# Local attention in a transformer stack: dividing the probabilities ahead of their transposes, and weighing with the values stationary

## The chip, the cores and the metric

One core of a Trainium2 chip runs the whole program in one launch. The metric is the device time of one execution in microseconds (us); several executions give a median.

## The reference

The input x has 2048 tokens of 128 features in float32. The program computes x + 0.5 F(norm(x)), adds a linear-attention block of 16 heads with its own feed-forward part, and then adds 0.5 F again. F is a stack of 6 layers, run twice with the same weights, so there are 12 layer passes. What matters here is the attention of such a layer, with 16 heads of 64 dimensions and windows of 32 tokens, each of which looks at itself and at the window before:

```python
qkv = x @ Wqkv                      # x: tokens, its upper 64 features shifted by one token
q, k, v = sh(q), sh(k), sh(v)       # 16 heads of 64
q = l2norm(q) * qs; k = l2norm(k) * ksc
q, k = rotary(q), rotary(k)
sim = einsum('bhwie,bhwje->bhwij', bq, bk2) * 8.0   # 32 queries against 64 keys
attn = softmax(where(mask, -max, sim), -1)
out = einsum('bhwij,bhwje->bhwie', attn, bv2)
x = out.reshape(b, n, 1024) @ Wo + x
```

Behind it stand a layer norm, a gated feed-forward part of 341 hidden units, and a residual.

## The kernel before

Activations live in SBUF for the whole run with features on partitions (XA, XB: 128 x 2048). A layer's attention works through 16 chunks (CH) of 128 tokens. It is pipelined by hand over steps: in step i every engine's function `step(p, i, ...)` does part a for chunk i (projection), part b for chunk i-1 (rotation, scores), part cc for the chunk whose scores are now complete (softmax, transposes of the probabilities, first weighing) and part d for the chunk before (rest of weighing, output projection). Chunks 0 to 2 start the layer without all parts, and steps 16 to 18 (`within`, `norm_before`) end it with parts b, cc, d alone, beside the layer norm of the feed-forward part that follows. The order on each engine is written out in these functions, and engines meet at semaphores that count chunks: `wait_ge(name, c(k))`. `dve.drain()` makes VectorE wait for its own writes.

The parts that the change and the prediction speak of, by engine:

- TensorE (PE): `project` multiplies the chunk's tokens, split in a high and a low part (XH, XL), by the split weights, three passes for each half of q, k, v (L382 to L384). It needs XL (`xs_ready`). `turn` makes 128x128 transposes (L390): of V (the rotated q and k), of PR (the probabilities; lines 492 to 499, both in banks TQ and TK), and of ON (the divided result; line 458). `score` gives the logits of two heads of a pair (r = 0, 1), four windows each (L406). `weigh` multiplies the transposed probabilities PT by the values V2: the probabilities are loaded, the values stream, and the result has tokens on partitions, in bank OB for r = 0 and OB + 1 for r = 1 (L416). Its eight head pairs stand in four blocks of two: 0 to 3 in the step of the transposes around the last half of the value projection, 4 to 7 in the next step around the first projection. The output projection multiplies OT by WO (L466).
- ScalarE (ACT), in this order in a step: copy and square of q (L697, L699, RAWQK and SQ), the copy of the transposed result OT (L732), copy and square of k, the copies of the transposed q and k (QT L703, KT L706), the exponential (L743, PR from SM), the second copies, the halo of the keys, the copies of the transposed probabilities PT (L755, L756, wait for `pt_ready`), XH of the next chunk (`shift`, L692 and L693), the values VS (L710).
- VectorE (DVE), in this order: the division of the weighed result by the probabilities' sums (L968, ON), the second product of the rotation (`rotate(1)`, L934), the sum of squares of q (L950), the row maximum and its subtraction (MX L979, SM L981), the sum of squares of k, the residual (XB, L988), the inverse norms by a short iteration on 32 columns (L871 to L890), QN (L927, twice), XL of the next chunk (`rest`, L943 and L945, wait for XH), the sums of the probabilities (L998) and their reciprocals (L1002), the first product of the rotation (`rotate(0)`, L934).
- GpSimd (POOL): the other products of the rotation, four on QN (L1185), and two additions (L1191, L1193) that need DVE's `rotate(0)` and `rotate(1)`.
- SyncE (SP): weights, and the 16 copies of a chunk's values into V2, where each window has its own 64 keys.

## Time and profile before

| | |
|---|---|
| median of 2 runs | 4887.01 us (4881.81 and 4892.21) |
| span of the profiled execution, first to last instruction | 4869.5 us |
| TensorE matmul busy | 3785.1 us, 78% |
| VectorE busy | 3828.5 us, 79% |
| ScalarE busy | 2483.4 us, 51% |
| GpSimd busy | 2389.1 us, 49% |
| mean granted TensorE clock | 0.905 of 2.4 GHz |

All durations of the profile come from one profiled execution, whose time is known by its span alone; the median of the runs lies 17.5 us above that span. In rows, "x4" is the number of merged instructions, and brackets hold the idle time of the engine before the row with what ended it. Matmuls are pipelined, so rows of PE overlap.

### The profile page before, as it was taken

What the parts mean: (1) busy time and instruction counts of PE and PEld (TensorE: products, weight loads), DVE (VectorE), ACT (ScalarE), POOL (GpSimd) and SP (SyncE); (2) the same over time, 40 slices, a digit from 0 to 9 for tenths busy, and PEclk for the clock granted to TensorE, in tenths of its full rate; (3) what the DMA queues carried; (4) which work ended last, traced back from release to release, by engine and by line L of the source; (5) the groups of instructions that cost most, each with busy time, mean ns of one, the idle gap of its engine ahead of it and who ended that gap; (6) DMA issues with size and microseconds to landing.
All of it is one profiled execution on the core that took longest, in us unless ns stands there. A gap on an engine that the chain in (4) does not pass through costs nothing.

```text
span 4869.5 us, 152986 instructions
## 1 busy us (share of the span) xinstructions
PE 3785.1 (78%) x64080; PEld 2581.5 (53%) x64080; DVE 3828.5 (79%) x6082; ACT 2483.4 (51%) x3705; POOL 2389.1 (49%) x1426
## 2 busy tenths in 40 slices
PE   5887887787787787788777877877877887887887
PEld 3554554554555455456435645554554554554554
DVE  4886886896896897797448878877976886986896
ACT  3554554554554565455225545554554554553553
POOL 3663563563664564455006535544553653553552
PEclk9998899899899999888878989999988998998999
DMA  2221221221221222122002212221221221221221
GB/s 82 54 57 46 53 55 48 53 54 44 58 56 51 49 57 58 40 55 63 6 10 51 57 47 51 56 57 43 57 58 39 55 59 40 57 55 44 53 57 46
DMA packets 179337, 247.34 MB, mean 51 GB/s; under 512 B 52516, under 2 KB 75040, under 8 KB 177184
## 3 DMA queue, kind: packets, MB, share of 16 engines
q1 hardware_dynamic: 178976, 242.09, 19.6%
q8 instruction: 281, 4.60, 0.4%
q14 instruction: 80, 0.66, 0.0%
HBM read 39.51 MB, written 1.05 MB: 8 GB/s over the span
## 4 chain that ended last, share of the span: by engine, by line
PE 35%; POOL 18%; DVE 17%; ACT 10%; issue 8%; DVEq 7%; SPq 3%; DMA 1%; ACTq 0%; POOLq 0%
POOL V L1185 9%; PE PS L390 6%; PE PS L544 5%; POOL V L1191 5%; POOL V L1193 5%; PE PS L382 4%; PE PS L466 3%; PE PS L416 3%; DVEq L1000 3%; DVE QN L927 3%; PE PS L383 2%; PE PS L384 2%; DVEq L921 2%; PE PS L576 2%; ACT PR L743 2%
## 5 line engine op out<-in xcount | busy, mean ns | idle before, releaser
L1185 POOL TENSOR_TENSOR V<-QN,TAB 128x512 f32<-128x512 f32 x768 | 1116.7, 1485 | 1791.2 <-DVE QN L927 1791.2
L382 PE MATMUL PS<-WH,XH 128*128 128x512 f32 x1152 | 634.4, 551 | 427.8 <-DVE XL L945 338.8
L697 ACT ACTIVATE RAWQK<-PS 128x1024 f32<-128x1024 f32 x384 | 392.3, 1022 | 848.5 <-PE PS L384 808.1
L934 DVE TENSOR_TENSOR U<-QN,TAB 128x1024 f32<-128x1024 f32 x384 | 736.8, 1922 | 16.4 <-issue 15.3
L390 PE MATMUL PS<-EYE,V 128*128 128x128 f32 x3072 | 449.6, 285 | 188.0 <-POOL V L1193 107.8
L1191 POOL TENSOR_TENSOR V<-V,U 128x1024 f32<-128x1024 f32 x192 | 516.6, 2690 | 81.3 <-DVE U L934 60.8
L382 PEld LDWEIGHTS PS<-WH,XH 128*128 128x128 f32 x1152 | 241.5, 210 | 560.4 <-DVE XL L945 210.3
L1193 POOL TENSOR_TENSOR V<-V,U 128x1024 f32<-128x1024 f32 x192 | 453.6, 2362 | 140.4 <-DVE U L934 140.4
L390 PEld LDWEIGHTS PS<-EYE,V 128*128 128x128 f32 x3072 | 366.1, 147 | 276.6 <-POOL V L1193 139.8
L384 PE MATMUL PS<-WL,XH 128*128 128x512 f32 x1152 | 511.2, 444 | 0.0
L383 PE MATMUL PS<-WH,XL 128*128 128x512 f32 x1152 | 511.0, 444 | 0.0
L950 DVE TENSOR_REDUCE SS<-SQ 128x16 f32<-128x1024 f32 x384 | 463.9, 1209 | 23.6 <-ACT SQ L699 23.6
L927 DVE TENSOR_TENSOR QN<-RAWQK,RN 128x1024 f32<-128x1024 f32 x384 | 453.4, 1222 | 15.1 <-issue 0.4
L703 ACT ACTIVATE QT<-PS 128x512 f32<-128x512 f32 x384 | 229.4, 597 | 460.6 <-PE PS L390 460.6
L416 PEld LDWEIGHTS PS<-V,PT 64*32 64x32 f32 x24576 | 264.3, 118 | 372.8 <-issue 372.8
L416 PE MATMUL PS<-V,PT 64*32 64x64 f32 x24576 | 388.3, 244 | 85.1 <-issue 80.1
L466 PE MATMUL PS<-OT,WO 128*128 128x128 f32 x3072 | 417.3, 292 | 35.1 <-ACT OT L732 29.3
L466 PEld LDWEIGHTS PS<-OT,WO 128*128 128x128 f32 x3072 | 379.3, 201 | 67.6 <-ACT OT L732 67.5
L699 ACT ACTIVATE SQ<-RAWQK 128x1024 f32<-128x1024 f32 x384 | 406.9, 1060 | 12.2
L406 PE MATMUL PS<-KT,QT 64*32 64x64 f32 x24576 | 388.9, 233 | 2.6 <-issue 2.6
L968 DVE TENSOR_TENSOR ON<-PS,SUM 128x1024 f32<-128x1024 f32 x192 | 235.2, 1225 | 161.8 <-PE PS L416 153.5
L732 ACT ACTIVATE OT<-PS 128x1024 f32<-128x1024 f32 x192 | 197.0, 1026 | 309.5 <-PE PS L390 309.5
(150 smaller groups left out, 6509.1 us busy)
## 6 DMA issues: line engine op xcount, KB each, us to landing
V<-VS SPq DMA_DIRECT2D x3072, 64.0 KB, 2.0
U<-wqkv SPq DMA_DIRECT2D x13, 1024.0 KB, 5.2
V<-wqkv SPq DMA_DIRECT2D x13, 512.0 KB, 6.8
WO<-wo SPq DMA_DIRECT2D x13, 512.0 KB, 3.8
W<-w SPq DMA_DIRECT2D x12, 341.0 KB
ROT<-c_rot SPq DMA_DIRECT2D x1, 2048.0 KB, 10.4
QKS<-qks SPq DMA_DIRECT2D x13, 128.0 KB, 3.7
W<-w SPq DMA_DIRECT2D x12, 114.0 KB
```

The lines of the kernel that those rows point to most:

```text
L382: pe.matmul(o, XH[:, p, :], WH[:, w], start=True, stop=False)
L383: pe.matmul(o, XL[:, p, :], WH[:, w], start=False, stop=False)
L384: return pe.matmul(o, XH[:, p, :], WL[:, w], start=False, stop=True)
L390: mm = pe.matmul(PS[:, bank, at:at + P], src(pair), EYE[:, :], is_transpose=True, start=True, stop=True, skip_group_check=True)
L416: mm = pe.matmul(PS[WIN * w:WIN * (w + 1), OB + r, j * DH:(j + 1) * DH], PT[DH * r:DH * (r + 1), j, WIN * w:WIN * (w + 1)], V2[DH * r:DH * ...
L466: mm = pe.matmul(PS[:, OB, 0:P], WO[:, h, :], OT[:, h, :], start=(h == 0), stop=(h == NP_ - 1))
L927: ins = dve.tensor_tensor(QN[:, k], RAWQK[:, k], rep(RN[:, k, :], [P, HEADS, DH], 2), ALU.mult)
L934: dve.tensor_tensor(paired(U[:, k]), split(QN[:, k]), per_dim(TAB[:, 2 * k * DH:(2 * k + 1) * DH], DH), ALU.mult).then_inc((u_q, u_k)[k], 1)
L950: dve.tensor_reduce(SS[:, k * HEADS:(k + 1) * HEADS], SQ[:, k], AX.X, ALU.add)
L1185: ins = pool.tensor_tensor(paired(V[:, k])[:, :, :, h * half:(h + 1) * half], split(QN[:, k])[:, :, :, (1 - h) * half:(2 - h) * half], per ...
L1191: pool.tensor_tensor(V[:, 0], V[:, 0], U[:, 0], ALU.add).then_inc(rot_q, 1)
L1193: pool.tensor_tensor(V[:, 1], V[:, 1], U[:, 1], ALU.add).then_inc(rot_ready, 1)
```

## The change

- DVE divides the probabilities and not the result. Behind QN it sums PR, takes the reciprocals, drains, and multiplies PR (128 x 1024) in place; this signals `pn_ready`. Only then comes XL (`rest`), then `rotate(0)`. The division L968 at the step's start is gone, and so is the drain at its end.
- PE waits for `pn_ready` instead of `e_ready` ahead of PR's transposes.
- `weigh` loads the values (64 x 64) and streams the transposed probabilities (64 x 32). The result has the dimension on partitions and the tokens in columns; r = 0 fills partitions 0 to 63 and r = 1 partitions 64 to 127 of the same bank, OB for pairs 0 to 3 and OB + 1 for pairs 4 to 7. The eight transposes of ON and the semaphores `on_ready`, `to_ready`, `rs_ready` are gone.
- ACT copies OT straight from the weighing's banks, once `o_ready` is there.
- WO is loaded in two transfers of 64 partitions, in the order of heads that fits.

```diff
--- before.py
+++ after.py
@@ -131,7 +131,6 @@
         PT = sb("PT", [P, NP_, P])
         VS = sb("VS", [P, 2, HEADS * DH])
         V2 = sb("V2", [P, 2, NW, NP_ * DH])
-        ON = sb("ON", [P, HEADS, DH])
         OT = sb("OT", [P, NP_, P])
 
 
@@ -189,7 +188,7 @@
         t0_ready = sem("t0_ready"); t1_ready = sem("t1_ready")
         tevq = sem("tevq"); tevq1 = sem("tevq1"); tev0 = sem("tev0"); tev1 = sem("tev1"); halo_ready = sem("halo_ready")
         s_ready = sem("s_ready"); sm_ready = sem("sm_ready"); e_ready = sem("e_ready")
-        rs_ready = sem("rs_ready"); on_ready = sem("on_ready"); to_ready = sem("to_ready")
+        pn_ready = sem("pn_ready")
         pt_ready = sem("pt_ready"); ptev = sem("ptev")
         v2_even = sem("v2_even"); v2_odd = sem("v2_odd")
         o_ready = sem("o_ready"); otev = sem("otev"); wo_ready = sem("wo_ready"); xb_ready = sem("xb_ready")
@@ -217,7 +216,7 @@
 
             return 1 + 4 * DEPTH * inv
 
-        A_DMAS, W_DMAS, F_DMAS, V2_DMAS = 2, 2, 4, 16
+        A_DMAS, W_DMAS, F_DMAS, V2_DMAS = 3, 2, 4, 16
         V2_INC = 16 * V2_DMAS
 
         def split(ap):
@@ -413,9 +412,10 @@
                 for j in pairs:
                     for w in range(NW):
                         for r in range(2):
-                            mm = pe.matmul(PS[WIN * w:WIN * (w + 1), OB + r, j * DH:(j + 1) * DH],
+                            at = (j % 4) * P + WIN * w
+                            mm = pe.matmul(PS[DH * r:DH * (r + 1), OB + j // 4, at:at + WIN],
+                                           V2[DH * r:DH * (r + 1), p, w, j * DH:(j + 1) * DH],
                                            PT[DH * r:DH * (r + 1), j, WIN * w:WIN * (w + 1)],
-                                           V2[DH * r:DH * (r + 1), p, w, j * DH:(j + 1) * DH],
                                            start=True, stop=True, skip_group_check=True)
                 return mm
 
@@ -453,9 +453,6 @@
                 if a:
                     pe.wait_ge(cp_q, c(1))
                     project(1, p, 0)
-                if d:
-                    pe.wait_ge(on_ready, c(-2))
-                    turn(lambda h: ON[:, 2 * h:2 * h + 2, :].rearrange("p r d -> p (r d)"), both).then_inc(to_ready, 1)
                 if a:
                     project(1, p, 1).then_inc(raw_k, 1)
                 if cc:
@@ -489,7 +486,7 @@
                     turn_qk(1, [1]).then_inc(t1_ready, 1)
                     score(q, range(0, 2))
                 if cc:
-                    pe.wait_ge(e_ready, c(-1))
+                    pe.wait_ge(pn_ready, c(-1))
                     pe.wait_ge(v2_odd if p else v2_even, v2(-2))
                     if b:
                         pe.wait_ge(tevq1, c(0))
@@ -728,8 +725,8 @@
                         act.wait_ge(qn_ready, c(0))
                     raw(0, raw_q, cp_q, sq_q)
                 if d:
-                    act.wait_ge(to_ready, c(-2))
-                    act.activation(OT[:, :, :].rearrange("p (b j) t -> p b (j t)", b=2), PS[:, TQ:TQ + 2, :],
+                    act.wait_ge(o_ready, c(0))
+                    act.activation(OT[:, :, :].rearrange("p (b j) t -> p b (j t)", b=2), PS[:, OB:OB + 2, :],
                                    ACT.Copy).then_inc(otev, 1)
                 if a:
                     raw(1, raw_k, cp_k, sq_k)
@@ -739,7 +736,6 @@
                     act.wait_ge(sm_ready, c(-1))
                     if past(i, 3):
                         act.wait_ge(pt_ready, c(-2))
-                        act.wait_ge(rs_ready, c(-2))
                     act.activation(paired(PR[:, :, :]), split(SM[:, :, :]), ACT.Exp,
                                    scale=QK_SCALE).then_inc(e_ready, 1)
                 if b:
@@ -962,11 +958,6 @@
                         dve.drain()
                         rotate(0, c(1))
                     return
-                if d:
-                    dve.wait_ge(o_ready, c(0))
-                    rsum = SUM[:, :].rearrange("p (j r) -> p r j", r=2).unsqueeze(3).broadcast_to([P, 2, NP_, DH])
-                    dve.tensor_tensor(split(ON[:, :, :]), PS[:, OB:OB + 2, :].rearrange("p r (j d) -> p r j d", d=DH),
-                                      rsum, ALU.mult).then_inc(on_ready, 1)
                 if b:
                     rotate(1, None)
                 if within and not cc:
@@ -991,21 +982,22 @@
                     within()
                 if a:
                     normalise(i, c)
-                if a and not (isinstance(i, int) and i == CH - 1):
-                    rest(2, i * P + P, 1 - p)
                 if cc:
                     dve.wait_ge(e_ready, c(-1))
                     dve.tensor_reduce(SUM[:, :], PR[:, :, :], AX.X, ALU.add)
                 if a or cc:
                     dve.drain()
                 if cc:
-                    dve.reciprocal(SUM[:, :], SUM[:, :]).then_inc(rs_ready, 1)
+                    dve.reciprocal(SUM[:, :], SUM[:, :])
+                    dve.drain()
+                    dve.tensor_tensor(PR[:, :, :], PR[:, :, :], rep(SUM[:, :], [P, HEADS, 2 * WIN], 2),
+                                      ALU.mult).then_inc(pn_ready, 1)
+                if a and not (isinstance(i, int) and i == CH - 1):
+                    rest(2, i * P + P, 1 - p)
                 if a:
                     if past(i, 1):
                         dve.wait_ge(rot_ready, c(0))
                     rotate(0, c(1))
-                if cc:
-                    dve.drain()
 
             def norm_before(inv, lay, g):
                 if g == 0:
@@ -1216,7 +1208,10 @@
                 sp.dma_start(W_IN[2], a["wqkv"][bass.ds(lay, 1), :, 2 * n:3 * n].rearrange("l p n -> p (l n)")).then_inc(w_in, 16)
 
             def load_attn(lay):
-                sp.dma_start(WO[:, :, :], a["wo"][bass.ds(lay, 1)].rearrange("l (h p) n -> p (l h) n", p=P)).then_inc(attn_w, 16)
+                for r in range(2):
+                    sp.dma_start(WO[DH * r:DH * (r + 1), :, :],
+                                 a["wo"][bass.ds(lay, 1), r * NP_ * DH:(r + 1) * NP_ * DH].rearrange(
+                                     "l (j d) n -> d (l j) n", d=DH)).then_inc(attn_w, 16)
                 sp.dma_start(QKS[:, :], a["qks"][bass.ds(lay, 1), :].broadcast_to([P, 4 * DH])).then_inc(attn_w, 16)
 
             def load_ffn(lay):
```

On DVE, from the steady loop's first step, between the scaling QN and the rotation U. Before:

```order
L927 TENSOR_TENSOR QN<-RAWQK,RN 128x1024 [waits vv_ready]
L927 TENSOR_TENSOR QN<-RAWQK,RN 128x1024
L942 REGISTER_ALU
L943 ISA [waits xs_high]
L943 TENSOR_TENSOR XL<-XA,XH 64x128
L945 ISA
L945 TENSOR_TENSOR XL<-XA,XH 64x128
L998 TENSOR_REDUCE SUM<-PR 128x16 [waits e_ready]
L1002 RECIPROCAL SUM<-SUM 128x16
```

The same place of the changed kernel:

```order
L923 TENSOR_TENSOR QN<-RAWQK,RN 128x1024 [waits vv_ready]
L923 TENSOR_TENSOR QN<-RAWQK,RN 128x1024
L987 TENSOR_REDUCE SUM<-PR 128x16 [waits e_ready]
L991 RECIPROCAL SUM<-SUM 128x16
L993 TENSOR_TENSOR PR<-PR,SUM 128x1024
L938 REGISTER_ALU
L939 ISA [waits xs_high]
L939 TENSOR_TENSOR XL<-XA,XH 64x128
L941 ISA
L941 TENSOR_TENSOR XL<-XA,XH 64x128
L930 TENSOR_TENSOR U<-QN,TAB 128x2x8x64 [waits tab_ready,rot_ready]
```

XL, which PE's next projection waits for, has moved behind the sums, the reciprocals and the new product PR; the wait for XH (`xs_high`) moved with it.

On PE, in the same step, around the output's way to the projection by WO. Before:

```order
L416 MATMUL PS<-V,PT 32x64 x16
L406 MATMUL PS<-KT,QT 32x64 x16
L382 MATMUL PS<-WH,XH 128x512 [waits cp_q]
L383 MATMUL PS<-WH,XL 128x512
L384 MATMUL PS<-WL,XH 128x512
L390 MATMUL PS<-EYE,ON 128x128 [waits on_ready]
L390 MATMUL PS<-EYE,ON 128x128 x7
```

The same place of the changed kernel:

```order
L416 MATMUL PS<-PT,V 64x32 x16
L405 MATMUL PS<-KT,QT 32x64 x16
L381 MATMUL PS<-WH,XH 128x512 [waits cp_q]
L382 MATMUL PS<-WH,XL 128x512
L383 MATMUL PS<-WL,XH 128x512
L381 MATMUL PS<-WH,XH 128x512
L382 MATMUL PS<-WH,XL 128x512
L383 MATMUL PS<-WL,XH 128x512
```

The transposes of ON and their wait have left, and the weighing streams 32 columns out of PT where it streamed 64 out of V2.

## Rows read from the trace of the kernel before

**Rows 1.** The page's head: the span, and busy time with its share of it.

```profile
span 4869.5 us, 152986 instructions
PE 3785.1 (78%) x64080; PEld 2581.5 (53%) x64080; DVE 3828.5 (79%) x6082; ACT 2483.4 (51%) x3705; POOL 2389.1 (49%) x1426
```

**Rows 2.** Line L998 in one layer's steps; busy time by stretch (window, length, engines).

```profile
L998 DVE TENSOR_REDUCE SUM<-PR x14: 1212/1220/1221, 488.5 to 739.6; 128x16 f32<-128x1024 f32 x14
...
488.50:739.60 251.10, 208.57 (x4177) 150.96 (x4177) 224.16 (x323) 146.08 (x218) 145.30 (x88) 0.90 0.23 55
```

**Rows 3.** Waits of the whole run: who waited for whom, us, times, longest.

```profile
PE PS L382 <- DVE XL L945: 338.8, 171, 2.8
DVE ON L968 <- PE PS L416: 153.5, 138, 3.4
DVE XL L943 <- ACT XH L693: 50.0, 57, 2.3
```

**Rows 4.** Timeline of a step, DVE and POOL: start, length in us, instruction.

```profile
712.87 1.23 DVE L979 TENSOR_REDUCE MX<-PS 128x16 f32<-128x1024 f32 x1 [0.74 <-PE PS L406]
...
719.55 2.36 DVE L927 TENSOR_TENSOR QN<-RAWQK,RN 128x1024 f32<-128x1024 f32 x2
...
721.83 0.28 DVE L943 TENSOR_TENSOR XL<-XA,XH 64x128 fp32r<-64x128 f32 x1
722.04 6.01 POOL L1185 TENSOR_TENSOR V<-QN,TAB 128x512 f32<-128x512 f32 x4 [7.78 <-DVE QN L927]
...
723.49 1.22 DVE L998 TENSOR_REDUCE SUM<-PR 128x16 f32<-128x1024 f32 x1
...
724.95 1.97 DVE L934 TENSOR_TENSOR U<-QN,TAB 128x1024 f32<-128x1024 f32 x1
...
727.01 1.22 DVE L968 TENSOR_TENSOR ON<-PS,SUM 128x1024 f32<-128x1024 f32 x1
```

**Rows 5.** The same step on PE and ACT.

```profile
718.38 1.06 PE L390 MATMUL PS<-EYE,PR 128*128 128x128 f32 x8 [0.39 <-ACT QT L703]
...
719.48 0.60 ACT L755 ACTIVATE PT<-PS 128x512 f32<-128x512 f32 x1 [0.15 <-PE PS L390]
...
720.76 0.31 ACT L693 ACTIVATE XH<-XA 64x128 fp32r<-64x128 f32 x1
...
723.51 0.50 PE L382 MATMUL PS<-WH,XH 128*128 128x512 f32 x1 [1.59 <-DVE XL L945]
...
724.40 0.46 PE L416 MATMUL PS<-V,PT 64*32 64x64 f32 x32
...
724.79 0.50 PE L382 MATMUL PS<-WH,XH 128*128 128x512 f32 x1
...
725.80 1.02 ACT L697 ACTIVATE RAWQK<-PS 128x1024 f32<-128x1024 f32 x1 [2.46 <-PE PS L384]
...
728.29 1.09 PE L390 MATMUL PS<-EYE,ON 128*128 128x128 f32 x8 [0.45 <-DVE ON L968]
...
730.00 0.46 PE L406 MATMUL PS<-KT,QT 64*32 64x64 f32 x32
```

**Rows 6.** Timeline of PE, the output projection in the step before.

```profile
691.75 2.05 PE L466 MATMUL PS<-OT,WO 128*128 128x128 f32 x16
```

**Rows 7.** Busy time by stretch of 4 us; PEclk is the granted clock.

```profile
core 0: us, PE busy (x) PEld busy (x) DVE busy (x) ACT busy (x) POOL busy (x), PEclk, DMA share, GB/s
700.00:704.00 4.00, 1.87 (x86) 1.10 (x67) 3.46 (x4) 2.44 (x6) 2.82 (x3) 0.96 0.00 0
704.00:708.00 4.00, 3.92 (x53) 2.25 (x61) 3.24 (x3) 0.05 (x1) 2.84 (x3) 0.50 0.00 0
```

**Rows 8.** Timeline of the layer's last steps, chunks 17 and 18.

```profile
769.27 1.09 PE L390 MATMUL PS<-EYE,PR 128*128 128x128 f32 x8 [0.23 <-ACT PR L743]
...
778.32 1.21 DVE L998 TENSOR_REDUCE SUM<-PR 128x16 f32<-128x1024 f32 x1
...
782.17 0.86 PE L416 MATMUL PS<-V,PT 64*32 64x64 f32 x64
```

## The prediction

> **What bounds the kernel now.** I read the page's totals first: VectorE (DVE) is busy for 79% of the span and TensorE (PE) for 78% [rows 1]. These are averages over two kinds of stage, so I took the table by stretches next. One layer's steps from chunk 2 to chunk 15 hold 14 row sums (L998), first at 488.5 and last at 739.6 us: 13 steps of 251.1 / 13 = 19.3 us, in which DVE is busy for 224.16 of 251.10 us (89%), PE for 83%, ACT and POOL for 58% [rows 2]. The rest of a layer (tail, feed-forward part, head of the next layer) is not touched by the edit but for its last steps. The timeline of a step shows why 89% is as good as all: one DVE instruction follows the other with gaps of 0.05 to 0.1 us, and the table of waits has little for DVE: 153.5 us in the whole run for the weighing matmuls and 50.0 us for the tokens' copy XH [rows 3]. What DVE waits for little, PE waits for more: 338.8 us for DVE's XL, the low part of the next chunk's tokens [rows 3]. So the step is DVE's own queue, with two roads beside it that nearly fill the same time: DVE XL to PE to ACT to DVE, and POOL's rotation.
>
> **What leaves DVE, and what enters it.** Out goes the division of the result, one instruction of 1.22 us a step (L968) [rows 4]. In comes the multiplication of PR by the reciprocals, also 1024 elements a partition. The trace has no such instruction, but a near one: the rotation L934 stands behind the same pair, sum and reciprocal, with two operands from SBUF, and beside POOL's L1185. From the start of the sum at 723.49 to that product's end (724.95 + 1.97) are 3.43 us [rows 4]. Free of POOL such a product takes 1.22 (QN: two in 2.36 us [rows 4]), so the new one costs between 1.22 and 2.0; I take 1.97, since L1185 starts as soon as QN is done. Of the XL pair the first took 0.28 us ahead of POOL's start, and both together, from 721.83 to the sum at 723.49, 1.66 [rows 4]; they now fall behind POOL's four products (6.01 us from 722.04), and at 0.28 each get back some 1.0. Added up, DVE's work stays as it was: -1.22 +1.97 -1.0, below 0.3 us a step. The DVE sum therefore predicts no change. The order of the queue does.
>
> **The new ring of waits.** PE's eight transposes of PR waited for the exponential alone, and ran at 718.38, while DVE was still at the norm; ACT copied PT, then XH, and XH was ready at 721.07, ahead of the end of QN at 721.91 [rows 4, 5]. Now PR is ready only after QN, sum, reciprocal and product. ACT's order is unchanged: PT's two copies stand ahead of XH, and DVE's XL needs XH. So DVE's next instruction behind the product waits for a road through PE and ACT that starts with the product. Count from the end of QN (Q = 0):
> - product done at 3.4 plus 0.1 for the second drain: 3.5.
> - PE transposes to ACT's first copy: 718.38 to 719.48 = 1.10, and 0.1 of start: 4.7. PT and XH, L755 to the end of L693: 719.48 to 721.07 = 1.6: 6.3 [rows 5].
> - DVE has idled 2.8 us. XL, two of 0.28: 7.0. Before, XL ended 1.6 us behind QN (721.91 to 723.49 [rows 4]).
> - PE is late too: weighing of pairs 0 to 1 from 5.5 (first PT copy at 5.3), project, pairs 2 to 3, and with the prices of the next part this ends at 8.0, so the next step's first projection starts there and not at 7.0.
> - From that start to ACT's copy: 723.51 to 725.80 = 2.3, plus 0.4 for the dearer weighing between: 10.7. The copy (1.02) and the square behind it, of the same size, end 2.1 later: 12.8 [rows 5].
> - DVE has done its two rotations (2.4 us) by 9.4 and idles 3.4 us more, up to the first sum of squares.
> - The scores: copy at 725.80 to the end of the scores at 730.46 are 4.7; without the eight ON transposes (1.09, of which the next block overlaps 0.2) 3.8: 14.5. DVE's maximum starts at 14.6.
> - From the maximum's start to the end of QN: 712.87 to 721.91 = 9.0 [rows 4]. Nothing in this piece changes. Sum: 23.6 us a step, against 19.3: +4.3.
>
> Two checks on it. The two idle pieces of DVE are 2.8 and 3.4 us, 6.2 together; before, DVE had 27 us in 13 steps, 2.1, so +4.1 beside the sum's small change. And the parts that the edit takes away (ON, its transposes 1.06 us of PE, ACT's copy 2.3 us sooner) are in the sum already: they shorten the road to the scores by 0.9 and otherwise end in idle time. POOL: rotation L1191 now starts at about 9.5 where it started at 6.3, but its two products end at 14.3, ahead of the scores; not the last wait. The V2 copies start with the weighing's end and have the whole next step; not the last either.
>
> **The weighing matmuls.** Both forms are 64 matmuls a step, each seen as two records, 32 records for two pairs of heads. Before, a record loads 32 columns and streams 64 in one of 8 tiles of the array, and 32 of them take 0.39 us from the start of the one to that of the next block (724.40 to 724.79; 12 ns each) [rows 5]. Afterwards it loads 64 and streams 32, and only two tiles are in use. The trace doesn't show that form. Bounds: 0.39 for 32 if the issue sets the pace; above, the Wo matmuls pay 2.05 us for 16 records of 128 + 128 columns, 0.5 ns a column [rows 6], so 96 columns are 48 ns: 1.5 us for 32 if the two tiles take turns, 0.77 if they run side by side. I take 0.8, which is +0.4 for each block of two pairs. Four blocks a step; three of them lie on the ring, as counted above. At 0.39 the step is 22.4 (+3.1).
>
> **PE's clock.** PE had 1.87 us of work in the stretch 700 to 704 us, and ran at a granted 0.50 of full speed (1.2 GHz) from 704 to 708 [rows 7]. After the change PE has nothing to do from its last score block (about 3.5 us ahead of Q) to the product: 7 us in each step. I expect a stretch at 1.2 GHz behind it in most steps, where now there are some. The transposes and the next blocks then take up to twice their time, at most 1.5 us a step; against that, the 19.3 of before contains such stretches and my durations are of 2.4 GHz. I take +0.4.
>
> **Tail.** At chunk 17 PR is transposed at 769.27, right behind the exponential, while DVE is in the layer norm until its sum starts at 778.32 [rows 8]. The transposes now come behind that sum: 778.32 + 2.9 (product free of POOL) = 781.2, then transposes and PT 2.2, weighing 1.6: the last weighing, at 782.17 before [rows 8], comes some 6 us later. Where the result is waited for, the chain is 2.4 us shorter in each of three steps (division 1.22, transposes 1.1). With chunks 15 and 16, where the product is in the road but no XL: +13 - 7 = +6 a layer, between 2 and 9.
>
> **Sum.** A layer: 13 x (4.3 + 0.4) + 6 = 67.1 us; 12 layers: 805. The profiled execution has a span of 4869.5 us [rows 1]; the median of the two runs is 17.5 above this, which I keep: 4869.5 + 805 + 17.5 = 5692, so 5690 us. Wo in two transfers: the feed-forward part covers it, 0.
>
> **Rivals.**
> 1. *One bank for both row halves* (6185 us, 0.12). Weighing wrote r = 0 and r = 1 to different PSUM banks; now both halves of the rows write to one bank. If they must take turns, 32 records take 1.5 us, not 0.8. On the ring: PE's backlog ends at 9.5, not 8.0, and the next blocks add 1.5 more: step 26.6 + 0.4, so 13 x 7.7 + 8 = 108 a layer, 4887 + 1298 = 6185. For it: nothing in this trace has two row halves in one bank, the scores avoid it too. Against it: the halves lie in different partitions and different columns of the array. The Trainium skill, TensorEngine Tiling, Gotcha 1, says that different row tiles can't access the same bank at the same time; by that the sum would be this one. No row here shows it.
> 2. *Shorter chain wins* (4650 us, 0.03). Were XH copied before the PR transposes are waited for, no new idle time would arise: DVE would lose its waits for the weighing (153.5 us [rows 3]) and the tails 3 x 2.4 x 12 = 86: -240. It decides if ACT's copy of XH doesn't wait for PT. Against it: XH stands behind PT in ACT's queue.
> 3. *DVE's sum stays the bound* (4890 us, 0.03): the new waits fall in idle time. For this the ring must stay under 19.3 us; my sum has 4.3 more.
> The rest, 0.82, is the ring. Its own range: 13 x 3.1 + 2 = 42 a layer (5395) with cheap weighing and no clock loss, up to 13 x 6.3 + 9 = 91 (5980) with weighing at 1.1 and the clock at 1.5.
>
> **Chances.** Faster by over 2% (about what a measurement can tell from no change) 0.03, within 2% 0.03, slower 0.94. Range 5400 to 5980: it leaves out rival 1 and a little at either end.
>
> **What would show it.** Right: step of 23.5 to 24.5 us between row sums; DVE idle before XL, released by ACT XH, of 2.5 to 3.5 us each; DVE idle before the first sum of squares; PE idle ahead of the PR transposes, released by DVE PR; POOL's L1191 waiting for U. Wrong: XL without a wait; two pairs of weighing at 0.4 us (then 5500) or 1.5 us (rival 1); a product of 1.2 us; a step that stays near 19.3.

## The result, and the profile after

The changed kernel took 7054.56 us (median of 2 runs, 7050.47 and 7058.64), the kernel before 4887.01 us (4881.81 and 4892.21). The ratio is 1.444, interval 1.439 to 1.449: slower by 2167 us. The forecast was 5690 us with a range up to 5980: the sign was right, and the size was 2.7 times too small.

The page of the changed kernel: its span, the busy time of the engines, the granted clock in 40 slices, and the chain that ended last.

```profile
span 7048.7 us, 149939 instructions
...
PE 5270.5 (75%) x62544; PEld 3930.8 (56%) x62544; DVE 3561.6 (51%) x6082; ACT 2496.7 (35%) x3705; POOL 2510.9 (36%) x1426
...
PEclk7667667667666766766876676666667667667667
...
PE 60%; DVE 24%; DVEq 8%; issue 4%; POOL 2%; ACT 1%; DMA 0%; SPq 0%; ACTq 0%; POOLq 0%
PE PS L416 20%; PE PS L381 8%; PE PS L389 6%; DVE PR L993 6%; PE PS L382 5%; PE PS L383 5%; PE PS L405 4%; PE PS L541 4%; DVEq L917 3%; DVE QN L923 3%; DVE SUM L987 3%; DVEq L989 3%; PE PS L463 3%; DVE MX L970 2%; DVE SM L972 2%
```

DVE has 267 us less to do than in [rows 1] and falls from 79% to 51% of the span. PE has 1536 matmul records fewer (the transposes of ON) and is busy for 1485 us more, with a clock of 0.6 to 0.8 in every slice; its mean is 0.686 where it was 0.905. The last chain now runs through PE for 60% of the span, and the weighing L416 alone holds a fifth of it. A kernel that was bound by DVE's queue is bound by a slow PE.

The same layer's steps as in [rows 2], by the row sums (now L987) and by the window from the first to the last of them:

```profile
L987 DVE TENSOR_REDUCE SUM<-PR x14: 1209/1211/1214, 671.6 to 1086.5; 128x16 f32<-128x1024 f32 x14
...
671.60:1086.50 414.90, 314.71 (x4108) 247.57 (x4108) 205.39 (x327) 148.89 (x221) 158.63 (x91) 0.65 0.14 33
```

A step takes (1086.5 - 671.6) / 13 = 31.9 us, forecast 23.6 + 0.4, before 19.3. Over all 12 layers the mean step went from 19.2 to 31.7 us and the rest of a layer (tail, feed-forward part, head) from 135.5 to 155.2: 12 x (13 x 12.5 + 19.7) = 2186, which is the whole difference but for 1%. So two numbers have to be explained, +12.5 a step (forecast +4.7) and +19.7 a layer (forecast +6).

The waits of the whole run, as in [rows 3] (who waited for whom, us in all, times, longest):

```profile
PE PS L389 <- DVE PR L993: 1415.3, 192, 9.7
DVE SS L946 <- ACT SQ L696: 1349.5, 176, 8.7
DVE XL L939 <- ACT XH L690: 630.2, 168, 4.1
...
PE PS L381 <- DVE XL L941: 35.2, 16, 3.0
```

The first three are those that the prediction named: PE for the product, DVE for XH (3.8 us each, forecast 2.8), DVE for the first square (7.7 us each, forecast 3.4). The wait of PE for XL that led [rows 3] is down to 35.2 us. The ring exists; it is longer than forecast. Where it is longer, a step shows (timeline of DVE, ACT and PE; compare [rows 4, 5]):

```profile
797.41 2.36 DVE L923 TENSOR_TENSOR QN<-RAWQK,RN 128x1024 f32<-128x1024 f32 x2 [0.15 <-issue]
...
801.30 2.15 DVE L993 TENSOR_TENSOR PR<-PR,SUM 128x1024 f32<-128x1024 f32 x1
803.75 1.94 PE L389 MATMUL PS<-EYE,PR 128*128 128x128 f32 x8 [7.96 <-DVE PR L993]
...
805.73 0.60 ACT L751 ACTIVATE PT<-PS 128x512 f32<-128x512 f32 x1 [8.59 <-PE PS L389]
...
806.42 1.92 PE L416 MATMUL PS<-PT,V 64*64 64x32 f32 x32
...
807.49 0.28 DVE L939 TENSOR_TENSOR XL<-XA,XH 64x128 fp32r<-64x128 f32 x1 [4.03 <-ACT XH L690]
...
808.27 0.79 PE L381 MATMUL PS<-WH,XH 128*128 128x512 f32 x1
...
816.81 1.02 ACT L694 ACTIVATE RAWQK<-PS 128x1024 f32<-128x1024 f32 x1 [6.26 <-PE PS L383]
...
818.95 1.22 DVE L946 TENSOR_REDUCE SS<-SQ 128x16 f32<-128x1024 f32 x1 [8.48 <-ACT SQ L696]
...
822.81 1.23 DVE L970 TENSOR_REDUCE MX<-PS 128x16 f32<-128x1024 f32 x1 [2.64 <-PE PS L405]
```

From the end of QN (797.41 + 2.36 = 799.77, the Q of the forecast) the product is done at 3.7 (forecast 3.5), ACT's first PT copy starts at 6.0 (4.7), the copy of q at 17.0 (10.7), the maximum at 23.0 (14.6). From the maximum to the end of QN stay 8.9 us (9.0). Up to the product and behind the maximum, on DVE, the forecast holds; all 8.4 us that are missing lie where PE works. The eight transposes of PR take 1.94 us where they took 1.06, a block of 32 weighing records 1.85 us to the start of the next (806.42 to 808.27) where 0.39 were before, and the first projection pass 0.79 where it took 0.50. The table by stretches of 4 us (columns as in [rows 7]) tells why:

```profile
796.00:800.00 4.00, 0.00 (x0) 0.00 (x0) 3.55 (x8) 1.04 (x3) 0.09 (x1) 1.00 0.20 49
804.00:808.00 4.00, 3.88 (x70) 3.33 (x71) 0.50 (x2) 2.17 (x5) 1.81 (x2) 0.50 0.00 0
808.00:812.00 4.00, 4.00 (x43) 3.12 (x41) 2.44 (x3) 0.60 (x1) 2.59 (x1) 0.50 0.00 0
812.00:816.00 4.00, 4.00 (x37) 3.09 (x37) 0.00 (x0) 0.00 (x0) 3.72 (x3) 0.50 0.00 0
816.00:820.00 4.00, 4.00 (x68) 3.02 (x68) 1.05 (x1) 2.99 (x3) 0.00 (x0) 0.50 0.03 7
820.00:824.00 4.00, 4.00 (x43) 2.89 (x43) 1.36 (x2) 1.85 (x2) 0.00 (x0) 0.50 0.44 108
824.00:828.00 4.00, 4.00 (x33) 3.48 (x31) 3.53 (x10) 1.98 (x4) 0.00 (x0) 0.99 0.41 99
```

PE idles for 7.96 us ahead of the product (the bracket at 803.75), and the granted clock falls to 0.50 (1.2 GHz). That was forecast. Not forecast was the rest: with PE busy for 4.00 of 4.00 us, the clock stays at 0.50 from 804 to 824, and is back only when the ring has passed PE. The step shown is no exception: in 152 of the 156 steps of all layers the trace has the clock back only behind the last of the four weighing blocks. Two readings were possible: the clock makes the blocks slow, or the new form of weighing is slow by itself (one bank, two tiles), and the clock only goes with it. The experiments were to tell these apart.

### The profile page after: what moved, and what is told of

Read it like the earlier page. It is cut to its first block, busy times and chain, and to the rows that moved or that the text cites. A ratio compares the mean times of both kernels' runs of the same rounds, so it can differ in the third digit from the quotient of the medians.

```text
span 7048.7 us, 149939 instructions
## 1 busy us (share of the span) xinstructions
PE 5270.5 (75%) x62544; PEld 3930.8 (56%) x62544; DVE 3561.6 (51%) x6082; ACT 2496.7 (35%) x3705; POOL 2510.9 (36%) x1426
## 3 DMA queue, kind: packets, MB, share of 16 engines
q1 hardware_dynamic: 179184, 242.09, 13.6%
HBM read 39.51 MB, written 1.05 MB: 6 GB/s over the span
## 4 chain that ended last, share of the span: by engine, by line
PE 60%; DVE 24%; DVEq 8%; issue 4%; POOL 2%; ACT 1%; DMA 0%; SPq 0%; ACTq 0%; POOLq 0%
PE PS L416 20%; PE PS L381 8%; PE PS L389 6%; DVE PR L993 6%; PE PS L382 5%; PE PS L383 5%; PE PS L405 4%; PE PS L541 4%; DVEq L917 3%; DVE QN L923 3%; DVE SUM L987 3%; DVEq L989 3%; PE PS L463 3%; DVE MX L970 2%; DVE SM L972 2%
## 5 line engine op out<-in xcount | busy, mean ns | idle before, releaser
L1177 POOL TENSOR_TENSOR V<-QN,TAB 128x512 f32<-128x512 f32 x768 | 1144.5, 1521 | 3261.7 <-DVE QN L923 3261.7
L416 PEld LDWEIGHTS PS<-PT,V 64*64 64x64 f32 x24576 | 1333.6, 215 | 432.2 <-issue 432.2
L416 PE MATMUL PS<-PT,V 64*64 64x32 f32 x24576 | 1422.5, 287 | 31.9 <-issue 8.8
L389 PE MATMUL PS<-EYE,PR 128*128 128x128 f32 x1536 | 375.4, 426 | 1415.3 <-DVE PR L993 1415.3
L389 PEld LDWEIGHTS PS<-EYE,PR 128*128 128x128 f32 x1536 | 301.2, 224 | 1442.7 <-DVE PR L993 773.7
L381 PE MATMUL PS<-WH,XH 128*128 128x512 f32 x1152 | 783.9, 680 | 96.1 <-ACT RAWQK L694 52.1
L751 ACT ACTIVATE PT<-PS 128x512 f32<-128x512 f32 x192 | 114.6, 597 | 1549.0 <-PE PS L389 1549.0
L382 PE MATMUL PS<-WH,XL 128*128 128x512 f32 x1152 | 644.0, 559 | 0.0
L383 PE MATMUL PS<-WL,XH 128*128 128x512 f32 x1152 | 638.7, 554 | 0.0
L930 DVE TENSOR_TENSOR U<-QN,TAB 128x1024 f32<-128x1024 f32 x384 | 504.6, 1353 | 21.1 <-issue 14.8
L970 DVE TENSOR_REDUCE MX<-PS 128x16 f32<-128x1024 f32 x192 | 235.0, 1224 | 547.2 <-PE PS L405 546.6
L463 PEld LDWEIGHTS PS<-OT,WO 128*128 128x128 f32 x3072 | 416.8, 217 | 38.5 <-issue 24.6
```

The lines of the kernel that those rows point to most:

```text
L381: pe.matmul(o, XH[:, p, :], WH[:, w], start=True, stop=False)
L382: pe.matmul(o, XL[:, p, :], WH[:, w], start=False, stop=False)
L383: return pe.matmul(o, XH[:, p, :], WL[:, w], start=False, stop=True)
L389: mm = pe.matmul(PS[:, bank, at:at + P], src(pair), EYE[:, :], is_transpose=True, start=True, stop=True, skip_group_check=True)
L416: mm = pe.matmul(PS[DH * r:DH * (r + 1), OB + j // 4, at:at + WIN], V2[DH * r:DH * (r + 1), p, w, j * DH:(j + 1) * DH], PT[DH * r:DH * (r ...
L463: mm = pe.matmul(PS[:, OB, 0:P], WO[:, h, :], OT[:, h, :], start=(h == 0), stop=(h == NP_ - 1))
```

## The experiments

Most of the kernels below were timed once. The kernel before, timed beside them, took 4881 to 4904 us, so a difference of some 20 us between two of them says nothing. "Restart" is the start of PR's transposes behind PE's idle time.

### The parts alone

The product alone: the kernel before, with PR divided behind the reciprocals, XL behind it, and the weighing in its old form (L968 becomes a plain copy of the same size).

```diff
-                    pe.wait_ge(e_ready, c(-1))
+                    pe.wait_ge(pn_ready, c(-1))
...
                     dve.reciprocal(SUM[:, :], SUM[:, :]).then_inc(rs_ready, 1)
+                    dve.drain()
+                    dve.tensor_tensor(PR[:, :, :], PR[:, :, :], rep(SUM[:, :], [P, HEADS, 2 * WIN], 2),
+                                      ALU.mult).then_inc(pn_ready, 1)
+                if a and not (isinstance(i, int) and i == CH - 1):
+                    rest(2, i * P + P, 1 - p)
```

> The kernel before, with the changed kernel's order on DVE (sums, reciprocals, product on PR, then XL) and PR's transposes behind the product; the weighing keeps its old form, and ON is a plain copy instead of the division. Theory R (the ring of waits makes most of the loss, and the PE clock falls because of the idle time in it): step of 24 to 27 us, 5700 to 6100 us in all, granted clock in the steps under 0.8. Theory W (the new weighing form makes most of it, by its length and by holding PE's clock down): the ring alone as I had it, 22.4 us a step, about 5400 us, clock near 0.9.

The weighing alone: the changed kernel without the product; PE waits for the exponential again, and XL stands ahead of the sums. It leaves the division by the sums out altogether.

```diff
-                    pe.wait_ge(pn_ready, c(-1))
+                    pe.wait_ge(e_ready, c(-1))
...
-                    dve.reciprocal(SUM[:, :], SUM[:, :])
-                    dve.drain()
-                    dve.tensor_tensor(PR[:, :, :], PR[:, :, :], rep(SUM[:, :], [P, HEADS, 2 * WIN], 2),
-                                      ALU.mult).then_inc(pn_ready, 1)
-                if a and not (isinstance(i, int) and i == CH - 1):
-                    rest(2, i * P + P, 1 - p)
+                    dve.reciprocal(SUM[:, :], SUM[:, :]).then_inc(pn_ready, 1)
```

> The changed kernel without the product: PR goes undivided into its transposes right behind the exponential, XL stands ahead of the sums again, the weighing has its new form and OT comes straight from it. Left out of the computation: the division by the sums. Theory R: DVE stays the bound, blocks of 32 records take 0.9 us at 2.4 GHz, 19.3 to 21 us a step, 4850 to 5100 us. Theory W: the clock stays near 0.6 although no ring is there, blocks take 1.85 us, PE becomes the bound, 25 us a step or more, over 5900 us.

Measured: 5848.8 us for the product alone (before: 4884.0), 4821.1 us for the weighing alone. The first has the step (24.6 us) and the time that theory R expected; its clock is 0.84 in one layer's steps, between the two theories. The second is just below the 4850 to 5100 of theory R. A later set of runs timed the latter again:

> e2_weighing_only again, timed against the kernel before in three rounds. The single look gave 4821 us beside 4884; I expect a ratio of 0.985 to 0.990 with an interval clear of 1: the new form with neither ring nor division is slightly the faster, as DVE has one instruction of 1.22 us less a step and gets only 0.5 us of it.

4829.94 us against 4887.04: ratio 0.989, interval 0.986 to 0.992. Alone the parts cost +965 and -57 us, both in one kernel +2167. They don't add up, so some 1260 us belong to neither part but to the two together. The new form of weighing, whose DVE has lost an instruction of 1.22 us in each step, is a small gain where its clock is high; two rows of PE in the kernel with the weighing alone, one block and what follows it:

```profile
620.49 1.12 PE L416 MATMUL PS<-PT,V 64*64 64x32 f32 x32
...
621.54 0.46 PE L405 MATMUL PS<-KT,QT 64*32 64x64 f32 x32
```

At full clock a block takes 1.05 us from start to start: in the forecast's bounds (0.39 to 1.5), and 0.25 above its 0.8. In the kernel with the product alone, PE also idles, for 7.77 us ahead of the transposes at 766.46, and the clock also falls. But see when it is back (stretches of 4 us):

```profile
764.00:768.00 4.00, 1.54 (x8) 1.57 (x8) 2.13 (x1) 0.00 (x0) 4.00 (x3) 0.50 0.00 0
768.00:772.00 4.00, 3.88 (x102) 2.25 (x100) 1.76 (x3) 2.75 (x6) 0.52 (x1) 0.50 0.00 0
772.00:776.00 4.00, 3.67 (x104) 2.53 (x104) 0.93 (x2) 1.37 (x3) 2.37 (x1) 0.89 0.00 0
```

It rises in the stretch from 772, some 6.4 us behind the restart, with one or two of the four weighing blocks done (in 153 of 156 steps).

### The bank

The halves r = 0 and r = 1 of a block go to different banks again, and ACT's copy of OT becomes three.

```diff
-                            mm = pe.matmul(PS[DH * r:DH * (r + 1), OB + j // 4, at:at + WIN],
+                            mm = pe.matmul(PS[DH * r:DH * (r + 1), OB + (j // 4 + r) % 2, at:at + WIN],
...
-                    act.activation(OT[:, :, :].rearrange("p (b j) t -> p b (j t)", b=2), PS[:, OB:OB + 2, :],
+                    act.activation(OT[0:DH, :, :].rearrange("p (b j) t -> p b (j t)", b=2), PS[0:DH, OB:OB + 2, :],
+                                   ACT.Copy)
+                    act.activation(OT[DH:P, 0:4, :].rearrange("p j t -> p (j t)"), PS[DH:P, OB + 1, :], ACT.Copy)
+                    act.activation(OT[DH:P, 4:8, :].rearrange("p j t -> p (j t)"), PS[DH:P, OB, :],
```

> The changed kernel, but row half 1 of the weighing writes to the other of the two banks than row half 0, so that no two row halves share a bank at a time; ACT copies OT with three instructions. If turns at the shared bank make the block of 32 records 1.85 us: it falls to about 1.0 at the same clock, 4 blocks save 3.4 us a step, 6500 us. If the load of 64 columns into one of two tiles makes it: the block stays at 1.85 and the time within 1% of 7054, plus up to 1 us a step (7200) for ACT's instructions.

Measured: 7045.8 us, step 31.6, within the 1% expected if the bank doesn't matter. A block in it:

```profile
802.06 1.92 PE L416 MATMUL PS<-PT,V 64*64 64x32 f32 x32
```

It is the 1.92 us of the changed kernel. At full clock, as in the block below from the same kernel, there is no difference either: 1.12 us, as in the kernel with the weighing alone, which has one bank.

```profile
715.04 1.12 PE L416 MATMUL PS<-PT,V 64*64 64x32 f32 x32
```

Two row halves in one bank cost nothing that can be seen here. Rival 1 falls, though its time of 6185 us lay nearest to the result of all that were named.

### XH out of PT's way

XH is copied by ACT ahead of PT, and XL made ahead of the sums; first in the changed kernel, then in the one with the product alone.

```diff
+                if a and not (isinstance(i, int) and i == CH - 1):
+                    if past(i, 1):
+                        act.wait_ge(raw_v, c(0))
+                    shift(i * P + P, q)
                 if cc:
                     act.wait_ge(pt_ready, c(-1))
...
-                    shift(i * P + P, q)
```

> The changed kernel, with XH of the next chunk copied ahead of PT on ACT and XL ahead of the sums on DVE, so that the next projection no longer waits for the road through PR's transposes. Theory R: the ring through XL is gone; PE still does the blocks behind the product, but starts them with the next projection at hand: DVE's 4 us wait before XL gone, step down by 4 to 8 us, 5700 to 6400 us. Theory W: PE's own queue from the product to the scores (18 us at 1.2 GHz) is what counts, since the next projection stands behind the weighing in it: less than 1 us a step, 6900 us or more.

> e1_product_only with XH copied ahead of PT and XL ahead of the sums. If the wait of DVE's XL for XH (4 us a step) is part of what the ring costs: step down by 2 to 4 us, 5300 to 5550 us. If PE's queue behind the product is the road that counts (in e1 the next projection starts 1 us after XL is ready, behind the weighing): within 2% of e1's 5849, rather above.

Measured: 7230.8 us (176 above the changed kernel) and 6068.6 us (220 above the product alone, steps of 26.0 for 24.6). Neither step got shorter, as the second reading of each expectation has it; the second kernel is 3.8% slower, though, where at most 2% was expected. DVE in a step of the second:

```profile
612.13 2.36 DVE L927 TENSOR_TENSOR QN<-RAWQK,RN 128x1024 f32<-128x1024 f32 x2
614.41 0.28 DVE L943 TENSOR_TENSOR XL<-XA,XH 64x128 fp32r<-64x128 f32 x1
...
614.70 1.33 DVE L945 TENSOR_TENSOR XL<-XA,XH 64x128 fp32r<-64x128 f32 x1
...
617.70 1.74 DVE L1003 TENSOR_TENSOR PR<-PR,SUM 128x1024 f32<-128x1024 f32 x1
```

DVE's wait for XH, some 630 us in all in the changed kernel and in the one with the product alone, is all but gone (24 us are left in the first), and the step is longer. The two XL end 1.54 us behind QN, the second at 1.33 us beside POOL's first product, and the sum starts that much later; the product ends 4.95 us behind QN where it ended 3.67 without them. These 1.3 us are nearly the 1.4 of the step. The wait of DVE for XH was a true row and no part of the ring: what follows XL on PE stands behind PE's own backlog anyway.

### PE's idle time filled

If the idle time ahead of the product is what makes the clock fall, useless work in it must bring the time back. 28 matmuls of 512 bf16 columns stand ahead of PE's wait for the product; nothing reads what they write. First in the changed kernel, then in the one with the product alone, and in the changed one with half of them.

```diff
+                if cc and a:
+                    for _ in range(28):
+                        pe.matmul(PS[:, OB + 1, :], EYEB[:, :], rep(MASK[:, 0, :], [P, NP_, 2 * WIN], 1),
+                                  start=True, stop=True, skip_group_check=True)
                 if cc:
                     pe.wait_ge(pn_ready, c(-1))
```

> The changed kernel, with 28 matmuls of 512 columns without use (bf16, the mask, into the free bank OB + 1) between PE's last score block and its wait for the product, 6.0 us at 2.4 GHz, so that PE is busy where it was idle. Theory K (the idle time lets the clock fall, and the doubled times of all PE work lie on the ring): granted clock over 0.9, weighing blocks 1.05 us instead of 1.85, step 24.7 us by my sum with the measured block, 5700 to 5900 us. Theory L (the ring through waits and the longer weighing make it, the clock little): the time stays over 6700 us.

> e1_product_only with the same 28 useless matmuls at the same place. Theory K: clock over 0.9, step 22.5 to 23 us instead of 25, 5350 to 5550 us: the ring alone, at the full clock. Theory L: within 2% of e1's 5849, or above by the fill.

> The changed kernel with 14 useless matmuls instead of 28 in PE's idle time ahead of the product: at 2.4 GHz 3.0 of some 7 us are filled, 4 stay idle. If the clock falls whenever PE has some 4 us without work: it falls in nearly all steps, and once fallen stays for the rest of the step, 31 to 32 us a step, 6900 us or more. If it falls only in some of them: a mix of steps of 24.2 and 31 us, 6100 to 6800 us.

Measured: 6049.6 us with 28 in the changed kernel, 5657.6 us with 28 in the product alone, 6950.8 us with 14. The first two lie above what theory K expected (up to 5900 and up to 5550) and below what theory L had (over 6700, and within 2% of 5849); the third is as expected for a clock that falls in nearly all steps. The first is the proof: it differs from the changed kernel by more work on PE and nothing else, and it is 1005 us faster. Its steps are 24.1 to 24.4 us where the clock stays up (124 of 156), and 31 in the 32 where it fell nevertheless; these 32 are 32 x 6.8 = 218 us of the time, and without them it would have been in the expected range. They are a second proof inside one kernel: the same instructions, 6.8 us longer at the low clock. Timeline of a step:

```profile
610.54 2.36 DVE L927 TENSOR_TENSOR QN<-RAWQK,RN 128x1024 f32<-128x1024 f32 x2
...
614.44 2.16 DVE L997 TENSOR_TENSOR PR<-PR,SUM 128x1024 f32<-128x1024 f32 x1
616.65 1.09 PE L389 MATMUL PS<-EYE,PR 128*128 128x128 f32 x8 [1.84 <-DVE PR L997]
...
617.78 0.60 ACT L755 ACTIVATE PT<-PS 128x512 f32<-128x512 f32 x1 [7.78 <-PE PS L389]
...
618.47 1.12 PE L416 MATMUL PS<-PT,V 64*64 64x32 f32 x32 [0.35 <-issue]
...
624.31 1.12 PE L416 MATMUL PS<-PT,V 64*64 64x32 f32 x32
624.41 1.02 ACT L698 ACTIVATE RAWQK<-PS 128x1024 f32<-128x1024 f32 x1 [3.29 <-PE PS L383]
...
626.56 1.22 DVE L950 TENSOR_REDUCE SS<-SQ 128x16 f32<-128x1024 f32 x1 [4.19 <-ACT SQ L700]
...
627.91 1.22 DVE L974 TENSOR_REDUCE MX<-PS 128x16 f32<-128x1024 f32 x1
```

Here the forecast's road can be read off at full clock, from the end of QN at 612.90: product done 3.7 (forecast 3.5), PT 4.9 (4.7), copy of q 11.5 (10.7), square's sum 13.7 (12.8), maximum 15.0 (14.6), and 24.1 for the step (23.6). With 14 fillers 141 of 156 steps stay at 31 to 32.6 us and 15 drop to 25.4: with half of the idle time left, the clock still falls in most steps.

### The product ahead of QN

Sum, reciprocal and product stand inside the normalisation, ahead of QN; then the same with 18 fillers, since PE's idle time is shorter.

```diff
                 dve.drain()
+                if between is not None:
+                    between()
...
+                if a:
+                    normalise(i, c, divide if cc else None)
```

> The changed kernel, but DVE does the sums, reciprocals and product right behind the inverse norms and ahead of QN, so that QN (2.4 us) fills the time in which PE and ACT work on PR and PT, and the product does not meet POOL. PE's idle time falls from 8 to some 4 us. Theory K: clock falls in fewer steps, step 21.5 to 24 us, 5250 to 5650 us. Theory L: only the 2.4 us of position and 0.9 of contention are saved, 28.5 us a step, 6500 us.

> e8_product_before_qn with 18 useless matmuls of 512 columns (3.9 us at 2.4 GHz) in PE's idle time of 3.9 us ahead of PR's transposes. If the low clock alone separates e8 (28.5 us a step) from the ring's sum: granted clock over 0.9, weighing blocks 1.05 us, PE's four blocks and six projections behind the product some 6 us shorter: 22 to 23 us a step, 5350 to 5600 us, the fastest correct form with the new weighing. If e8's price lay in its order: over 6200 us.

Measured: 6510.1 us (28.5 a step), which is what theory L had and not the 5250 to 5650 of theory K; and with the fillers 5330.2 us (ratio 1.093, interval 1.089 to 1.096; 21.3 a step), just under the 5350 to 5600 that were expected. The product and PE behind it, without fillers:

```profile
709.37 1.23 DVE L991 TENSOR_TENSOR PR<-PR,SUM 128x1024 f32<-128x1024 f32 x1
...
710.65 1.97 PE L389 MATMUL PS<-EYE,PR 128*128 128x128 f32 x8 [3.92 <-DVE PR L991]
```

Ahead of POOL's start the product takes 1.23 us, not 2.15, and PE idles for 3.92 us. The transposes still take 1.97 us: behind 3.9 us of idle time the clock is at 1.2 GHz here too (at 184 of the run's 192 restarts). What failed in theory K was that a shorter idle time would spare the clock in most steps; that the clock is what separates this kernel from its ring, the fillers show: 28.5 us a step without them, 21.3 with them. The order on DVE was worth 545 us and not a cure. With both, the chain that ended last reads:

```profile
POOL V L1185 10%; PE PS L416 7%; PE PS L490 6%; PE PS L389 6%; POOL V L1191 5%; PE PS L545 5%; POOL V L1193 4%; PE PS L381 4%; PE PS L463 3%; DVEq L921 3%; DVEq L1002 3%; DVE SUM L991 3%; PE PS L383 2%; PE PS L382 2%; DVE XL L947 2%
```

L416 is down from 20% to 7%, and POOL's rotation leads again, as in a kernel bound by DVE and POOL. This is the fastest form found that divides PR, and it is 9% slower than the kernel before.

### What keeps the clock down

Two kernels to tell whether it is the new form of the blocks. In the first, 8 useless matmuls of 512 columns stand behind the first weighing block of the changed kernel, inside the ring. In the second, the product alone does each old-form pair three times, so that a block is about as long as one of the new form (3 x 0.39 = 1.17 us, 1.05).

```diff
                     weigh(p, range(0, 2))
+                    if a:
+                        for _ in range(8):
+                            pe.matmul(PS[:, OB + 1, :], EYEB[:, :], rep(MASK[:, 0, :], [P, NP_, 2 * WIN], 1),
+                                      start=True, stop=True, skip_group_check=True)
```

```diff
-                for j in pairs:
+                for j in [j for j in pairs for _ in range(3)]:
```

> The changed kernel with 8 useless matmuls of 512 columns on the full array behind the first weighing block, 3.4 us at 1.2 GHz, so PE has more to do on the ring and not less. If the clock stays low because the blocks of 64-column loads and 32-column streams pass for little work: the streams bring it back, the rest of the step runs at 2.4 GHz, and the step is 28 to 31 us, below the changed kernel's 31.7 in spite of the added work. If the low clock lasts for another reason (the length since the idle time): 3 us more a step, 35 us, 7500 us.

> e1_product_only with every weighing block done three times in its old form (same result), so that a block is as long as one in the new form: 1.8 us at 1.2 GHz, 1.2 us at 2.4. If the new form itself keeps the clock low: here the clock comes back some 7 us behind the product as in e1, step 27 to 28.5 us, 6200 to 6450 us. If the length of PE's queue does: clock low for the most of the step, 31 us or more, over 6900 us.

Measured: 6671.4 us for the first, with a mean step of 29.1 in the expected 28 to 31. It puts 3.60 us of work on the ring in each step, and is 383 us faster than the changed kernel:

```profile
704.88 1.94 PE L389 MATMUL PS<-EYE,PR 128*128 128x128 f32 x8 [7.96 <-DVE PR L997]
...
707.55 1.92 PE L416 MATMUL PS<-PT,V 64*64 64x32 f32 x32
...
709.40 3.60 PE L507 MATMUL PS<-MASK,EYEB 128*128 128x512 bf16 x8
...
713.99 1.12 PE L416 MATMUL PS<-PT,V 64*64 64x32 f32 x32
```

The block at 707.55 takes 1.92 us, the one at 713.99, behind the long streams, 1.12: the clock is back some 8 us behind the restart at 704.88, where it took 20 without them. The second kernel took 7038.4 us, where 6200 to 6450 were expected if the new form is the cause: by its time alone it would speak for the other reading, the length of PE's queue (over 6900). Its trace doesn't. In the stretches behind the transposes at 779.24 the clock is back within 6 us:

```profile
780.00:784.00 4.00, 3.88 (x135) 3.12 (x134) 0.98 (x3) 2.17 (x5) 1.29 (x2) 0.50 0.02 4
784.00:788.00 4.00, 4.00 (x198) 2.83 (x196) 0.82 (x1) 0.60 (x1) 2.38 (x1) 0.90 0.03 8
```

Its mean clock is 0.817 (after: 0.686), and in all 156 steps the clock is back after one or two blocks. It is slow for other reasons: its blocks are long at any clock, two thirds of its steps take 28 to 31.5 us and the others up to 37.5 (in many of these the clock falls a second time), and the rest of a layer takes 165.6 us; why the longest steps are so long was not looked into. The ON transposes, which this kernel has and the changed one hasn't, come only behind the clock's return (at 792.13) and don't explain it. So it isn't the amount of weighing that keeps the clock down. What stays is something in the new form: 64 columns loaded for 32 streamed, or two tiles of the array where there were eight. Which of these was not separated.

## Why the prediction was wrong, and where it was right

A step adds up over four kernels (in us; the first a mean, the others typical steps): 19.2 (before); 22.9 (the product alone with PE's idle time filled: the ring, at full clock, in the old form with its ON transposes); 24.2 (the changed kernel filled: the new form, +1.3, which is the dearer blocks less what the ON transposes and their wait took); 31.9 (the changed kernel: the clock, +7.7). At full clock the forecast's 23.6 is 0.6 short of 24.2.

- **Ring of waits: right.** +3.7 measured. The forecast's +3.1 with cheap blocks is without the ON transposes; with their 0.9 put back it is +4.0. The product moved off the exponential's heels was the right thing to look at.
- **Product, 1.97 us: right.** 2.15 us beside POOL's L1177, and 1.23 us in the kernel where it stands ahead of POOL.
- **Weighing block, 0.8 us: a little low.** 1.05 us at full clock, and 1.85 in the changed kernel, at 1.2 GHz. The sum had three blocks on the ring; the filled kernel's PE runs without a gap from the first block to the scores, so all four are (the fourth is the row at 624.31, ahead of the maximum at 627.91). Four at +0.66 are 2.6 us, where the forecast had 1.2; that the step came out within 0.6 all the same is partly luck: the piece from the copy of q to the maximum was forecast at 3.9 us with a cheap fourth block in it, and took 3.5 with the dear one.
- **Clock, "I take +0.4", "at most 1.5 us a step": the step that failed.** It measures +7.7. The fall itself was forecast, with the idle time that causes it (7 us forecast, 7.96 measured). Wrong was how long it lasts. The working doubled "the transposes and the next blocks" and took for granted that the clock is back behind them, as the one low stretch in [rows 7] seemed to say. What PE did there was of the old form, and even there the next stretch of the same table still has 0.68, so the low clock lasted some 6.5 us behind PE's restart at 704.09:

```profile
708.00:712.00 4.00, 4.00 (x78) 3.13 (x73) 3.37 (x3) 2.46 (x3) 2.68 (x2) 0.68 0.22 52
```

For the old form the 1.5 us would have been about right: the product alone takes 24.6 us a step, and 22.9 with the clock kept up, so 1.7. In the changed kernel the low clock lasts 20 of 31.9 us and doubles all that PE has on the ring. That is checked from two sides: with PE kept busy ahead of the product the 7.7 us are gone, and with old-form blocks behind the same idle time the clock is back in some 6 us (6.4 and 5.6 in the stretches shown). The upper end of 1.5 had only that assumption under it, and so the range was wrong with it: 156 steps x 7.3 = 1139 us, and with the other misses of a step 156 x 7.8 = 1217. With the tails' 12 x 13.7 = 164 that is 1381, against the 1364 us between 5690 and the 7054 measured. (The stated upper end has a slip besides: three blocks at 1.1 and the clock at 1.5 make 3.1 + 2.1 + 1.5 = 6.7 us a step and 6040 us, not 6.3 and 5980; and rival 1 is priced with four blocks on the ring, the sum with three. Neither would have reached 7054.)
- **Tail, +6 a layer: mis-sized.** +19.7 measured; +11.7 with the product alone, and +13.6 with the new form and fillers in the steps (which stand in steps with a projection only). PE idles ahead of the product there as well (8.84 us in the row below), and the weighing of four pairs behind it takes 3.62 us for 64 records, forecast 1.6:

```profile
1139.92 1.97 PE L389 MATMUL PS<-EYE,PR 128*128 128x128 f32 x8 [8.84 <-DVE PR L993]
...
1142.62 3.62 PE L416 MATMUL PS<-PT,V 64*64 64x32 f32 x64 [0.73 <-issue]
```

- **DVE's waits: right in place, short in size** (3.8 and 7.7 us for 2.8 and 3.4). For XH the wait doesn't matter at all, as moving XH showed; the prediction had XL in the ring only until PE's backlog passed it, which holds.
- **Rival 1, one bank: wrong.** The Trainium skill, TensorEngine Tiling (Array Packing), Gotcha 1, says that different row tiles cannot access one PSUM bank simultaneously. This case's runs don't agree as far as time goes: 1.92 us for a block with one bank or with two (1.12 at full clock), 7054.6 and 7045.8 us.
- **Rivals 2 and 3: wrong,** as their chances said. Rival 2 put its gain on XH being free of PT; made so, the kernel is slower.

The Trainium skill, TensorE: Matmul & The Clock Gate, Part 1, says that the half rate is the default and that sustained matmul activity lifts it. The traces agree with the first half as far as idle time goes (0.50 behind 7.96 us without work), and with the second only in part: in the changed kernel PE is busy for 4.00 of 4.00 us in four stretches on end, in three of them with new-form blocks in turn with projection passes, and the clock stays at 0.50; with eight long streams put between them it is back some 8 us behind the restart.

## What to carry to other kernels

An edit that makes PE wait in every period has two prices: the wait, and all that PE does afterwards at half the clock, until it is back. How long that is can't be read from a stretch with other matmuls in it: take as the upper bound that everything PE has on the ring runs at 1.2 GHz (here 24.2 + 7.7), and let the range reach there. To tell the two prices apart, fill PE's idle time with matmuls that nothing reads; and edits that meet on one engine, here short streams and a wait ahead of them, can't be priced apart and added.

## What the runs showed of the hardware that was not expected

- PE can be busy for 4.00 of 4.00 us in four stretches on end (in three of them with new-form weighing blocks in turn with projection passes) and keep the granted clock of 0.50; in 152 of 156 steps the clock rose only when the last of these blocks was done. Busy time in the table of stretches doesn't tell whether the clock will rise.
- Adding 3.60 us of work to the ring made the kernel 383 us faster, through the clock alone.
- In the kernel with the product ahead of QN, PE idled for only 3.92 us ahead of the transposes in the step shown, and they ran at 1.2 GHz (1.97 us); so they did at 184 of 192 restarts.
- Weighing with the values loaded (64 columns, 32 streamed, two tiles) takes 33 ns a record at 2.4 GHz and 58 ns at 1.2 GHz (1.05 and 1.85 us for 32), against 12 ns for the old form in eight tiles.
